# Attention stage of a one-core block: another order for the small products that share one PSUM bank

## The reference

```python
q = split(x @ Wq); k = split(x @ Wk); v = split(x @ Wv)
scores_dot = jnp.einsum('bihd,bjhd->bhij', q, k) * scale
q_amp = _amp_norm(q)   # a = softplus(t); a / sqrt(mean(a * a over the head) + 1e-6)
k_amp = _amp_norm(k)
q_phi = math.pi * jnp.tanh(split(x @ Wqp))
k_phi = math.pi * jnp.tanh(split(x @ Wkp))
scores_phase = (einsum(q_amp * cos(q_phi), k_amp * cos(k_phi))
                + einsum(q_amp * sin(q_phi), k_amp * sin(k_phi))) * scale
# scores = scores_dot + lam * scores_phase, causal softmax, times v, then @ Wo
```

## Time and profile before

| | |
|---|---|
| median of 3 runs | 1274.72 us (1273.44 to 1281.04) |
| profiled execution | 1278.36 us, of which the span of the core 1276.6 us |
| PE busy | 1093.0 us, 86% of the span |
| DVE / ACT / POOL busy | 906.5 (71%) / 656.6 (51%) / 267.2 (21%) us |
| granted TensorE clock, mean | 0.923 of full |
| steady loop of the attention | 611 to 1034 us of the span |

### The profile page before, as it was taken

The page is one execution under the profiler, slowest core; times in us unless marked ns, Lnnn a source line. Parts: engine busy times, 40 slices in busy tenths (PEclk is TensorE's granted clock), DMA queues, the critical chain, the costliest instruction groups (busy, mean ns, idle before and its releaser), DMA issues. The chain is left out here.

```text
span 1276.6 us, 16117 instructions
## 1 busy us (share of the span) xinstructions
PE 1093.0 (86%) x5200; PEld 649.7 (51%) x5200; DVE 906.5 (71%) x1927; ACT 656.6 (51%) x1204; POOL 267.2 (21%) x300
## 2 busy tenths in 40 slices
PE   3888889975999999776788888888888969999996
PEld 1223223324676667434455555555556636666774
DVE  2778998976877876874676666667766618787775
ACT  1234444425555555584556565665755546555553
POOL 1445565630000000220212111121212210000000
PEclk9789998977999999886698898989989989999999
DMA  5000000001232121439776767586755312323311
GB/s 192 0 1 1 0 0 1 0 1 46 88 119 81 67 71 63 102 129 259 248 183 141 204 165 193 137 205 169 170 141 136 61 67 67 134 67 99 101 67 66
DMA packets 45502, 129.04 MB, mean 101 GB/s; under 512 B 6512, under 2 KB 8560, under 8 KB 38768
## 3 DMA queue, kind: packets, MB, share of 16 engines
q1 hardware_dynamic: 43376, 127.53, 35.4%
q10 hardware_dynamic: 2048, 0.53, 0.2%
HBM read 88.72 MB, written 36.70 MB: 98 GB/s over the span
## 5 line engine op out<-in xcount | busy, mean ns | idle before, releaser
L1458 DVE TENSOR_REDUCE attn_maxima<-attn_ps_p 128x1 f32<-128x512 f32 (+3 forms) x235 | 146.0, 637 | 106.0 <-PE attn_ps_p L966 88.2
L1377 POOL TENSOR_SCALAR_AFFINE_SELECT attn_probs<-attn_probs 128x512 f32<-128x512 f32 x128 | 84.7, 696 | 321.8 <-ACT attn_probs L1210 321.8
L1835 ACT ACTIVATE moe_hidden<-moe_ps_h 128x512 f32<-128x512 f32 x128 | 76.3, 596 | 146.0 <-PE moe_ps_y L1773 144.3
L961 PE MATMUL attn_ps_p<-attn_stack 96*128 96x384 f32 (+3 forms) x341 | 121.3, 399 | 11.0 <-DVE attn_maxima L1458 10.0
L1957 DVE TENSOR_TENSOR moe_gated<-moe_ps_y,moe_gate_all 128x512 f32<-128x512 f32 x106 | 73.1, 690 | 75.2 <-issue 46.8
L1009 PE MATMUL attn_ps_q<-attn_stack 128*128 128x128 f32 (+3 forms) x343 | 108.8, 381 | 12.4 <-DMA attn_stack<-attn_neg_max 10.9
L1755 PE MATMUL moe_ps_h<-moe_x_high,moe_w_high 128*128 128x512 f32 x256 | 107.4, 420 | 0.0
L1458 DVE TENSOR_REDUCE attn_maxima<-attn_ps_t 128x1 f32<-128x384 f32 (+3 forms) x117 | 74.4, 636 | 44.1 <-PE attn_ps_t L966 41.8
L1757 PE MATMUL moe_ps_h<-moe_x_high,moe_w_low 128*128 128x512 f32 x256 | 102.8, 402 | 0.0
L1756 PE MATMUL moe_ps_h<-moe_x_low,moe_w_high 128*128 128x512 f32 x256 | 102.4, 400 | 0.0
L1771 PE MATMUL moe_ps_y<-moe_hidden_high,moe_w_low 128*128 128x512 f32 x128 | 101.0, 789 | 0.0
(11 more groups left out here) (256 smaller groups left out, 2426.8 us busy)
## 6 DMA issues: line engine op xcount, KB each, us to landing
moe_gate_all<-moe_gates SPq DMA_DIRECT2D x128, 256.0 KB, 4.9
attn_kept<-attn_parts SPq DMA_DIRECT2D x16, 1536.0 KB, 7.9
attn_stack<-attn_kept SPq DMA_DIRECT2D x64, 384.0 KB
attn_stack<-attn_kept SPq DMA_DIRECT2D x64, 192.0 KB
attn_value<-attn_values SPq DMA_DIRECT2D x5, 1792.0 KB, 12.3
attn_values<-attn_early SPq DMA_DIRECT2D x2, 1792.0 KB, 5.7
attn_values<-attn_probs SPq DMA_DIRECT2D x2, 1792.0 KB, 21.9
experts_in_w<-in_w SPq DMA_DIRECT2D x2, 1024.0 KB, 11.3
```

The costliest lines, as they stand in the source:

```text
L961: return mm(tiles(m)[:, i, :], stack[0][q][0:ROWS, h + i, t * P:(t + 1) * P], stack[1][q][0:ROWS, h + i, 0:(t + 1) * P], **flags)
L1377: nc.gpsimd.affine_select(out=tile, in_=tile, compare_op=ALU.is_ge, fill=0.0, base=0, pattern=[[0, 4], [1, P]], channel_multiplier=-1).the ...
L1458: nc.vector.tensor_reduce(maxima[:, u % 2, h:h + heads, t], tiles, AX_X, ALU.max).then_inc(g_free, 1)
```

## The change

The slots of the small work move. Nothing is computed otherwise, and no instruction is added or removed in the loop; the features' first steps now start in the batch before. The bank's order changes in one place: A0 goes from behind FW (slot 20) to between M0b and E1 (slot 5).

| step | slot before | slot now |
|---|---|---|
| PE: A0, FW, E0 | 20, 17, 28 | 5, 18, 29 |
| ACT side 0: size, exponential, log of sum | 4, 5, 7 | 33, 34, 36 of the batch before |
| ACT side 0: squares, log of mean, inverse | 12, 21, 22 | 0, 6, 7 |
| ACT side 0: high 0, 1, 2 | 14, 25, 29 | 9, 14, 16 |
| ACT side 1: size, exponential, log, squares | 8, 9, 11, 18 | 8, 10, 12, 18 |
| ACT side 1: high 0, 1, 2 (log of mean, inverse stay at 26, 27) | 16, 35, 37 | 20, 34, 36 |
| DVE side 0: softplus | 9 | 37 of the batch before |
| DVE side 0: amplitude, circle 1, circle 2 | 23, 25, 27 | 10, 11, 12 |
| DVE side 0: low 0, 1, 2 | 16, 28, 31 | 13, 16, 18 |
| DVE side 1: softplus, low 0 | 13, 20 | 15, 22 |
| DVE side 1: amplitude, circle 1, circle 2 | 32, 33, 35 | 30, 31, 32 |
| DVE side 1: low 1, 2 | 37, 39 | 36, 38 |
| DVE: splitting of maxima, in each quarter | 4 | 3 |
| DVE: add to x, normalise E0 | 18, 29 | 19, 30 |

```diff
     for b in range(NB):
         order += [("M0b", b)]
+        order += [("A0", b + 2)] if b + 2 < NB else []
         order += [("E1", b - 1)] if b else []
         order += [("M1a", b)]
         order += [("FT", b - 1), ("FW", b - 1)] if b else []
-        order += [("A0", b + 2)] if b + 2 < NB else []
         order += [("M1b", b)]
...
                 if b < LAST:
                     keep(b + 1, 1)
                     refill(b, 0, 0)
-                    refill(b, 0, 1)
                 if b + 3 < NB:
                     fetch(b + 3)
-                if b < LAST:
-                    refill(b, 1, 0)
                 if b + 2 < NB:
                     keep(b + 2, 0)
                 if b < LAST:
+                    refill(b, 0, 1)
+                    refill(b, 1, 0)
                     refill(b, 1, 1)
...
                 if b + 2 < NB:
                     features(b + 2, 20 * q + k)
+                if b + 3 < NB:
+                    features(b + 3, 20 * q + k - 40)
...
+            for k in range(-8, 0):
+                features(2, k)
```

More of the change, by code:

```diff
@@ L1076, in between @@
                     turn_normalised(b - 1)
-                if g == 1 and at == 7 and b:
+                if g == 1 and at == 8 and b:
                     project(b - 1)
-                if g == 2 and at == 0 and b + 2 < NB:
+                if g == 0 and at == 5 and b + 2 < NB:
                     mean("A0", b + 2)
@@ L1084, in between @@
                     turn_output("E1", b - 1)
-                if at == 8 and g == 2:
+                if at == 9 and g == 2:
                     turn_output("E0", b)
@@ L1237, in features @@
             def features(b, k):
-                if k == 4:
+                if k == -7:
                     size(b, 0)
-                if k == 5:
+                if k == -6:
                     exponential_of_size(b, 0)
+                if k == -4:
+                    log_of_sum(b, 0)
+                if k == 0:
+                    squares(b, 0)
+                if k == 6:
+                    log_of_mean(b, 0)
                 if k == 7:
-                    log_of_sum(b, 0)
+                    inverse(b, 0)
                 if k == 8:
@@ L1267, in features @@
                     inverse(b, 1)
-                if k == 29:
-                    high(b, 0, 2)
-                if k == 35:
+                if k == 34:
                     high(b, 1, 1)
-                if k == 37:
+                if k == 36:
                     high(b, 1, 2)
@@ L1488, in features @@
             def features(b, k):
-                if k == 9:
+                if k == -3:
                     softplus(b, 0)
+                if k == 10:
+                    amplitude(b, 0)
+                if k == 11:
+                    scale_circle(b, 0, 1)
+                if k == 12:
+                    scale_circle(b, 0, 2)
                 if k == 13:
+                    low(b, 0, 0)
+                if k == 15:
                     softplus(b, 1)
                 if k == 16:
-                    low(b, 0, 0)
-                if k == 20:
+                    low(b, 0, 1)
+                if k == 18:
+                    low(b, 0, 2)
+                if k == 22:
                     low(b, 1, 0)
-                if k == 23:
-                    amplitude(b, 0)
-                if k == 25:
-                    scale_circle(b, 0, 1)
-                if k == 27:
-                    scale_circle(b, 0, 2)
-                if k == 28:
-                    low(b, 0, 1)
+                if k == 30:
+                    amplitude(b, 1)
                 if k == 31:
-                    low(b, 0, 2)
+                    scale_circle(b, 1, 1)
                 if k == 32:
-                    amplitude(b, 1)
-                if k == 33:
-                    scale_circle(b, 1, 1)
-                if k == 35:
                     scale_circle(b, 1, 2)
-                if k == 37:
+                if k == 36:
                     low(b, 1, 1)
-                if k == 39:
+                if k == 38:
                     low(b, 1, 2)
@@ L1520, in between @@
                 g, at = 2 * q + k // 10, k % 10
-                if at == 4:
+                if at == 3:
                     if g == 0:
@@ L1529, in between @@
                         split_maxima("M0a", b + 1, 2 * b + 2)
-                if g == 1 and at == 8 and b:
+                if g == 1 and at == 9 and b:
                     add_output(b - 1)
@@ L1533, in between @@
                     normalise("E1", b - 1)
-                if at == 9 and g == 2:
+                if at == 0 and g == 3:
                     normalise("E0", b)
```

18 lines of the change are left out of this document (7 added, 11 removed).

## The result

| | before | after |
|---|---|---|
| median | 1277.58 us (1272.65 to 1283.72, 11 runs) | 1269.23 us (1261.65 to 1275.40, 11 runs) |
| ratio to before, 95% interval | | 0.9932 [0.9904, 0.9959] |
| span of the profiled execution | 1276.6 us | 1271.1 us |
| PE / DVE / ACT / POOL busy | 1093.0 / 906.5 / 656.6 / 267.2 us | 1094.8 / 914.8 / 658.0 / 269.9 us |
| granted clock, mean | 0.923 | 0.912 |

The kernel became faster by 0.7%, about 8.4 us by the medians. Forecast were 20.8. So the sign was right and the time lies in the range, but less than half of the gain came. Of the four executions of one later kernel, `r_pool_first`, two ran at a lower clock and over 1.5% above its fastest; comparisons with it use the other two.

The account below looks back on a forecast made before the run. It took third quarters as bound by engines waiting on each other, fourth by DVE, first stretched by a low clock. Terms, plus 1.0 for a softplus before the loop, summed to -20.8 us from 1274.72, so 1254; range 1238 to 1272.

Parts of the forecast that it names:

- 1 third quarter: Third quarters: moved slots loosen the ring of waits over three queues; -4.2 us in five batches, -2.5 in batch 0, -23.5 total.
- 2 first quarter: First quarters: A0's mean comes in and E1 also waits for A0's logarithm; +1.3 us a batch, +7.8 total.
- 3 second quarter: Second quarters: five more DVE instructions, covered by DVE's idle time; +0.3 us a batch, +1.8 total.
- 4 fourth quarter: Fourth quarters: DVE has six features before and now, ACT gets three more; 0, bounds -2 and +4 us.
- 5 waits at batch starts: Batch starts: PE's waits for first row maxima shrink as keep and fetch run in earlier quarters; -6.0 us.
- 6 clock: Loop's granted clock: half of the 13.8 us lost to its lower level should return; -6.9 us.
- 7 SP's order: SP's queue: second refill behind the keep comes 0 to 2.2 us late, taken as 1.0 in five batches; +5.0 us.
- M1a beside the fetch: Second row maxima of a half share DMA engines with the fetch; counted as nothing, send and use about 4.8 us apart.
- the clock stays as it is: Rival, chance 0.15: PE's short waits move to E1 and the lower clock remains as long as before; 1261 us.
- All goes well: Rival, chance 0.17: the clock stays up and the refill is in time; 1242 us.
- the second quarter becomes DVE's: Rival, chance 0.17: second quarter's five added DVE instructions lie uncovered, +18 us in place of +1.8; 1270 us.
- Slower: the stack half comes late: Rival, chance 0.13: keep and refill wait on the fetch, refill 6.4 us late in five batches, +48 us; 1297 us.

Follow-up runs that it names:

- r_pool_first: s_refill_first with POOL placing values ahead of zeroing the first quarter's probabilities, so the fetch can go earlier; 1245.39 and 1247.07 us, the other two 1265.38 and 1270.60.
- b_ring_only: Kernel before the change with only the third quarter's ring loosened, no feature step moved to the batch before, SP's order untouched; 1249.00 us, ratio 0.9744.
- s_refill_first: Changed kernel with the second refill put ahead of the keep of side 0 on SP's queue; 1245.45 us, ratio to before 0.9743.
- r_late: s_refill_first with the second refill held back until the keep's wait for DVE's low has ended; 1246.17 us, ratio 0.9751.
- padded kernels: HBM rows padded by 16 columns, so refills move 2 KB rows: on the changed kernel 0.9895, on s_refill_first 0.9796, on b_ring_only 0.9816.
- s_fetch_back: Changed kernel with only the fetch put back behind the second refill on SP's queue, the keep staying ahead of that refill; 1279.21 us, ratio 1.0006.

## Why the prediction was right in sign and wrong in size

| term | forecast | what the traces show |
|---|---|---|
| 1 third quarter | -4.2 a batch | -4.1 where nothing else disturbs (12.30 us in batch 5 against 16.37); -8.4 in sum, since the waits at slot 20 lie in these quarters |
| 2 first quarter | +1.3 a batch | +1.3 at full clock (13.40 in batches 1 and 4 against 12.08); E1 waits for nothing |
| 3 second quarter | +0.3 a batch | -1.0 (11.09 against 12.11), with DVE busy for 10.60 |
| 4 fourth quarter | 0 | -1.2 a batch (10.49 against 11.68) where no wait stands in it; DVE 9.55 us with 18 instructions, not 10.97 with 21 |
| 5 waits at batch starts | -6.0 | -6.8 (0 in batches 1 to 5; 8.4 us before, 1.6 after) |
| 6 clock | -6.9 | nothing: 0.93 before, 0.90 after in the same 435 us |
| 7 SP's order | +5.0 | stack half 2.1 to 4.3 us late in four batches, not 1.0, and the maxima with it: 17.6 us of waits at slot 30, and 9.4 more in the same quarters, at a fallen clock |
| M1a beside the fetch | 0 | 12.4 us of waits at slot 20 in five batches |

**What held.** Terms 1, 2 and 5 came to within a microsecond; term 1's ring is what one reads in the earlier trace rows, and `b_ring_only` shows that it can be had alone. Terms 3 and 4 were too cautious by 1.3 and 1.2 us a batch, together some 15 us. That the time still fell into the range is in part luck: these 15 us covered over half of what term 7 cost too much. Term 3 costed DVE's five more instructions (the trace has 19 in the quarter, not 21) and not what `b_ring_only` shows, that this quarter gets 1.0 us shorter from the small edits alone; which of these does it wasn't tried. Term 4 rested on counting features by slots, and the count of what DVE does in the quarter fell by three.

**What failed: term 7.** It had the right resource and the right pair of transfers, and two things wrong. The first is its own quantity, how late the stack half comes. The term set 14.1 us for the pair, or 11.1 by the rate, against a quarter of 11.9, as if the keep went at the quarter's start, and took 1.0 us out of 0 to 2.2. The keep goes 1.2 us into the quarter, the pair takes 14.3 to 15.6 us, and in a quarter of 12.3 (batch 5) to 13.7 (batch 3) the stack half is 2.1 to 4.3 us late. The second is what it left out: it asked only for the stack half, and the 16 KB of row maxima, which PE needs first at slot 30, landed only when keep and refill were through, 0.4 to 0.8 us behind the stack half. Which of the two costs the wait can be estimated from the semaphore events and the timeline. Had the maxima been there, PE would have made one slot's scores, some 0.6 us, and then stood for the stack half: 1.9, 4.1, 2.4 and 3.8 us by the arrivals seen, some 12 of the 17.6. So the maxima alone add a third, and to send them sooner would not have cured the quarter; the kernels with the refill ahead of the keep bring both in time. The price: in the fourth quarters of batches 1, 2, 3 and 5, waits of 3.29 + 5.49 + 3.60 + 5.22 = 17.6 us; the quarters take 15.07, 18.89, 17.61 and 17.43, which over 10.49 and these waits is 1.3, 2.9, 3.5 and 1.7 (sum 9.4), at clocks of 0.89, 0.73, 0.71 and 0.80. Together 27 us instead of 5. `s_refill_first` gives 24 us back (0.9932 to 0.9743 of 1278 us), by moving one line.

**The same error a second time** is the sentence "I count nothing, since send and use lie four slots apart, about 4.8 us". The row gave 4.2 us beside a fetch, but there the maxima were sent 8.2 us behind the fetch's issue (756.67 and 764.87), when most of it was through; now they are sent 1.1 to 1.9 us behind it and take 5.6 to 8.4. A landing time under load isn't a property of the small transfer. It depends on how much of the load is still ahead, and both of my uses of it took a row with less ahead. As I read the Trainium skill's rule that I set beside it (DMA: Bandwidth & Descriptors, Queues, rings and completion order: turns between queues, packet by packet), there would be none of these waits; the traces disagree with that reading more sharply than before, with 9.5 us against 1.8 and no packet of ACT's queue for 3.7 us. No run shows how much of a bulk transfer makes up one such turn, so it is the reading that fails, and the rule itself stays untested.

**Term 6** took for granted that the lower level goes with the waits at batch starts. It partly did: the first quarter of batch 4 has full clock and those of batches 2 and 3 have 0.89, where all three had 0.79 or 0.80. But behind the new waits it is low, 0.73 and 0.71 in the fourth quarters of batches 2 and 3 against 1.00 and 0.97 before, and it is 0.79 in batch 5's first, with no long wait just ahead of it. Of the rivals, *the clock stays as it is* (1261) so describes the clock's total, for another reason than it gave. In `r_late` the loop has 0.94.

**The other rivals.** *All goes well* needed a refill in time and is excluded by the waits; *the second quarter becomes DVE's* is excluded by 11.09 us. *Slower: the stack half comes late* had the chain fetch, keep, refill and the fallen clock behind it, at a price of 48 us. Its first link did not hold: in batches 1 to 4 the fetch had landed when the keep was issued, or did so within 1.1 us. Its end did, with the stack half 2.1 to 4.3 us late in place of 6.4, the maxima behind it, and 27 us in place of 48. It didn't tip the sign, because the slots were worth more than I gave them.

**Still open.** Why a small transfer on another queue lands only about when the bulk ahead of it does, and why refill and then keep are through sooner than keep and then refill. The size of the rows is not the cause, by the padded kernels; that the refill loads where the keep stores, that it is four transfers, and that the third refill is issued 4.1 us behind the sending of M1b were not told apart. It isn't a plain first come, first served either: in batches 1 to 4 of `s_fetch_back` M1b is sent 0.9 us behind a fetch and lands 4.3 to 4.8 us before it, 1.8 to 2.5 us behind the refill. Which of the seven edits of `b_ring_only` gives what, and whether its ring and the refill ahead of the keep add up in one kernel, was not tried.

## What to carry to other kernels

When a bulk transfer moves on a queue, list every small transfer that is sent while it is in flight, on other queues too, and take as its landing time the end of the bulk issued ahead of it, not the time that it took beside another load. Count that end from the bulk's real issue, wait and all, and ask of everything that the next step needs whether it is there, the bulk's own data and the small transfer's. A load that is needed next belongs ahead of a store that nobody waits for yet. And try the smallest part of a rearrangement by itself: seven small edits round one ring were worth as much as the best form of the whole.

## What the runs showed of the hardware

A pair of 8 KB transfers on ACT's queue lands in 1.8 us alone, and in 4.1 to 4.9 (batches 1 to 4 of `r_late`), 5.6 to 8.4 or 7.6 to 9.5 us (the changed kernel) beside a bulk on SP's queue, depending on how much of that is ahead of it at the sending. Sent 1.2 to 1.9 us behind a fetch, its second transfer landed within 0.3 us of the fetch (batches 1 to 4 of the changed kernel); sent behind keep and refill, 0.4 to 0.8 us after the refill, 14.7 to 16.4 us after the keep's issue. The exception is `s_fetch_back`, where it landed 4.3 to 4.8 us before a fetch issued 0.9 us ahead of it. In the first 3.7 us beside the refill none of its packets is seen. A keep and then a refill were through in 14.3 to 15.6 us, a refill and then a keep in 12.1 to 13.2 (`r_late`). The refill's stretch moved 157 to 195 GB/s with the engines' time nearly full, and 160 with its rows cut to 2 KB; the keep's moved 365. SP's own issue of a refill row took 0.3 to 0.4 us, but 1.0 to 1.2 in the second to fourth row behind a keep.
